# Cross-attention and FFN on one core: TensorE's program without alignment, v of the first pair and the FFN's weights in other space at other times, last pairs in another order

## What is computed

```python
def attn(hidden_q, hidden_kv, mask, position_bias, Wq, Wk, Wv, Wo):
    q = (hidden_q @ Wq).reshape(b, lq, h, dh)
    k = (hidden_kv @ Wk).reshape(b, lk, h, dh)
    v = (hidden_kv @ Wv).reshape(b, lk, h, dh)
    score = einsum('bqhd,bkhd->bhqk', q, k) / sqrt(dh) + position_bias
    probs = where(mask, softmax(where(mask, score, -inf)), 0)
    return einsum('bhqk,bkhd->bqhd', probs, v).reshape(b, lq, h * dh) @ Wo

def ffn(x, base_W, base_b, router_W, router_b, A, B, expert_map):
    base_out = x @ base_W.T + base_b
    probs = softmax(x @ router_W.T + router_b)
    topk_p, topk_i = top_k(probs, 8)
    w = einsum('btk,btke->bte', topk_p, expert_map[topk_i] == arange(8))
    h = einsum('btd,erd->bter', x, A)
    return base_out + 2 * einsum('bter,eor->bto', h * w[..., None], B)

x = x + attn(layernorm(x), ctx, ...)
x = x + ffn(layernorm(x), ...)
```

## Time and profile before

| | |
|---|---|
| three runs, us | 788.65, 790.44, 790.91 (median 790.44) |
| the profiled execution | 791.96 |
| its span, first to last instruction | 790.1 |
| TensorE matmuls, weight loads | 780.8 us (99%), 652.0 us (83%) |
| VectorE, ScalarE, GpSimd | 521.5 (66%), 399.9 (51%), 185.3 (23%) |
| chain that ended last | TensorE 93%, DMA 2%, VectorE 2%, SyncE's queue 1%, issue 1% |
| TensorE clock granted, mean | 0.998 |
| DMA | 118.40 MB, mean 150 GB/s |
| instruction packets of queue q8 | 52, 0.85 MB |

### The profile page before, as it was taken

The page is one execution under the profiler, slowest core; times in us unless marked ns, Lnnn a source line. Parts: engine busy times, 40 slices in busy tenths (PEclk is TensorE's granted clock), DMA queues, the critical chain, the costliest instruction groups (busy, mean ns, idle before and its releaser), DMA issues.

```text
span 790.1 us, 16795 instructions
## 1 busy us (share of the span) xinstructions
PE 780.8 (99%) x6360; PEld 652.0 (83%) x6360; DVE 521.5 (66%) x951; ACT 399.9 (51%) x1138; POOL 185.3 (23%) x203
## 2 busy tenths in 40 slices
PE   8999999999999999989999999999999999999998
PEld 7888888888888888878888888888888888887886
DVE  6883626267677665577666776676667676657974
ACT  5663525246556555573665456535654466435520
POOL 0225041024333434232222122212211221010200
PEclk9999999999999999999999999999999999999999
DMA  6536773245544547583564355534563355342002
GB/s 226 199 121 220 225 243 138 109 139 159 190 160 159 169 154 215 171 250 111 164 182 135 110 157 161 163 110 130 162 177 115 112 160 176 109 118 83 2 6 103
DMA packets 108078, 118.40 MB, mean 150 GB/s; under 512 B 44239, under 2 KB 77007, under 8 KB 107998
## 3 DMA queue, kind: packets, MB, share of 16 engines
q1 hardware_dynamic: 107998, 117.31, 47.7%
HBM read 81.64 MB, written 35.65 MB: 148 GB/s over the span
## 4 chain that ended last, share of the span: by engine, by line
PE 93%; DMA 2%; DVE 2%; SPq 1%; issue 1%; ACT 0%
PE pY L1393 42%; PE pP L1393 39%; PE pY L1552 4%; PE pO L1577 2%; PE pT_ L1577 2%; PE pS L1562 1%; DMA wv_raw<-in_L_xattn_Wv 1%; PE pO L1393 1%; PE pT_ L1562 1%; DMA v<-v_hbm 1%; DMA k_hbm<-stage 1%; SPq L425 1%; DVE st L980 1%; PE pS L1577 1%; DVE y L1129 0%
## 5 line engine op out<-in xcount | busy, mean ns | idle before, releaser
L1129 DVE TENSOR_TENSOR y<-y,pY 128x512 f32<-128x512 f32 x124 | 84.6, 682 | 24.6 <-PE pY L1393 24.2
L1393 PE MATMUL pY<-wo_hi,oT_hi 128*128 128x512 f32 x248 | 97.4, 393 | 1.2 <-issue 1.2
L1393 PE MATMUL pY<-wo_lo,oT_hi 128*128 128x512 f32 x248 | 97.2, 392 | 0.0
L1393 PE MATMUL pY<-wo_hi,oT_lo 128*128 128x512 f32 x248 | 97.2, 392 | 0.0
L910 DVE TENSOR_TENSOR wk_lo<-wk_raw,wk_hi 128x256 fp32r<-128x256 f32 x96 | 46.7, 487 | 62.2 <-ACT wk_hi L651 61.3
L759 ACT ACTIVATE pr<-pr,mx 128x64 f32<-128x64 f32 x256 | 86.2, 344 | 2.8 <-DVE mx L1146 2.8
L651 ACT CAST wk_hi<-twk 128x256 fp32r<-128x256 f32 x128 | 50.7, 409 | 64.5 <-PE pP L1393 53.6
L1393 PE MATMUL pP<-xo_hi,wk_hi 128*128 128x512 f32 x196 | 78.1, 399 | 0.0
L1393 PE MATMUL pP<-xo_hi,wk_lo 128*128 128x512 f32 x196 | 76.6, 391 | 0.0
L1393 PE MATMUL pP<-xo_lo,wk_hi 128*128 128x512 f32 x196 | 76.4, 390 | 0.0
L584 POOL TENSOR_TENSOR bias<-bias,madd 128x512 f32<-128x512 f32 x32 | 41.5, 1308 | 148.2 <-DMA bias<-in_fside_Bx32xSxS 148.2
(11 more groups left out here) (282 smaller groups left out, 1896.6 us busy)
## 6 DMA issues: line engine op xcount, KB each, us to landing
v_hbm<-stage SPq DMA_DIRECT2D x64, 256.0 KB, 2.3
k_hbm<-stage SPq DMA_DIRECT2D x64, 256.0 KB, 3.6
k<-k_hbm SPq DMA_DIRECT2D x16, 1024.0 KB, 5.1
v<-v_hbm SPq DMA_DIRECT2D x16, 1024.0 KB, 7.0
wk_raw<-in_L_xattn_Wk SPq DMA_DIRECT2D x16, 512.0 KB, 4.4
wo_raw<-in_L_xattn_Wo SPq DMA_DIRECT2D x16, 512.0 KB, 3.7
bias<-in_fside_Bx32xSxS SPq DMA_DIRECT2D x128, 64.0 KB, 3.6
wk_raw<-in_L_xattn_Wq SPq DMA_DIRECT2D x16, 512.0 KB, 4.7
```

The lines of the kernel that those rows point to most:

```text
L1129: nc.vector.tensor_tensor(y[:, t, :], y[:, t, :], src[:, :], ALU.add).then_inc(y_added, 1)
L1393: mm = nc.tensor.matmul(bank_, a, b, start=first and n == 0, stop=last and n == len(terms) - 1, skip_group_check=read_between)
```

## The change

It has four parts. The diff below goes, in order, through the tiles, SyncE, ScalarE (pair 14, then 15), VectorE and TensorE. (1) The five `addr_align` are gone; instead of 14 transposes of 128x128 the second warm-up has 12, and 26 of 32x32. (2) v of the first pair goes to a tile of its own, `v0`, over the context's space (read for the last time by product 4 of QA), so it waits for no store; the FFN's raw weights move to the same space and are loaded in passes 1 to 4 and not in passes 12 and 13 and ahead of pair 0, and VectorE's nine small operations on `mapi` move from pass 0 to pass 3. (3) `make_c21(QB)` stands ahead of `lower_wo(0)` on VectorE. (4) In pair 14 ScalarE's `exp(h + 2, 0)` stands behind its four `o_high`; in pairs 14 and 15 `ffn_weights(4)` and (5), and their splits, stand later.

```diff
+        v0 = at("v0", R0 + 16384, [P, NT, 2 * DH])
+        a_raw = at("a_raw", R0 + 16384, [P, D])
+        r_raw = at("r_raw", R0 + 18432, [NR, D])
+        b_raw = at("b_raw", R0 + 20480, [P, DC, ER])
+        bw_raw = at("bw_raw", R0 + 24576, [P, DC, D])
...
-        bw_raw = at("bw_raw", R1 + 49152, [P, DC, D])
...
-        a_raw = at("a_raw", R4 + 16384, [P, D])
-        r_raw = at("r_raw", R4 + 18432, [NR, D])
-        b_raw = at("b_raw", R4 + 20480, [P, DC, ER])
...
             def load_v(i):
-                sp.dma_start(v[:, :, :], v_hbm[i // 2, :, :, i % 2 * 2 * DH:(i % 2 + 1) * 2 * DH]
+                sp.dma_start((v if i else v0)[:, :, :], v_hbm[i // 2, :, :, i % 2 * 2 * DH:(i % 2 + 1) * 2 * DH]
...
+            sp.wait_ge(prod, DONE[QA, 4])
+            load_v(0)
+            store(QA, 2, c21_made)
             load_wk(QA - 9)
-            store(QA, 2, c21_made)
-            sp.wait_ge(prod, DONE[QA, 4])
-            sp.dma_start(bb[:, :], base_b.partition_broadcast(P)).then_inc(ld_small, 16)
-            sp.dma_start(rb[:, :], router_b.partition_broadcast(P)).then_inc(ld_small, 16)
-            sp.dma_start(mapi[:, :], emap.partition_broadcast(P)).then_inc(ld_small, 16)
-            for i in range(4):
-                sp.wait_ge(put[0][i], 16 * (QA // 2 + 1))
-            load_v(0)
...
                 sp.wait_ge(o_full, 4 * (i + 1))
+                if i == 0:
+                    for n in range(4):
+                        sp.wait_ge(put[0][n], 16 * (QA // 2 + 1))
                 load_v(i + 1)
-                if i == NP - 4:
-                    sp.wait_ge(w_lo[5], NSET - 1)
-                    sp.wait_ge(tw_made, 4 * (NSET - 1))
+                if i == 1:
+                    sp.dma_start(bb[:, :], base_b.partition_broadcast(P)).then_inc(ld_small, 16)
+                    sp.dma_start(rb[:, :], router_b.partition_broadcast(P)).then_inc(ld_small, 16)
+                    sp.dma_start(mapi[:, :], emap.partition_broadcast(P)).then_inc(ld_small, 16)
+                if i == 2:
                     sp.dma_start(a_raw[:, :], a_d).then_inc(ld_a, 16)
                     sp.dma_start(r_raw[:, :], router_W).then_inc(ld_a, 16)
-                if i == NP - 3:
-                    sp.wait_ge(prod, len(ORDER))
+                if i == 3:
                     sp.dma_start(bw_raw[:, :, :], bw_d).then_inc(ld_ffn, 16)
+                if i == 4:
                     for o in range(DC):
...
             turned_p(h + 1)
-            exp(h + 2, 0)
             o_high(h, 0)
             o_high(h, 1)
             o_high(h + 1, 0)
             o_high(h + 1, 1)
+            exp(h + 2, 0)
             exp(h + 2, 1)
...
             wo_high(NP - 1)
-            split_ffn(4)
             turned_p(h + 2)
             turned_p(h + 3)
-            split_ffn(5)
+            split_ffn(4)
             o_high(h + 2, 0)
...
             o_high(h + 3, 1)
+            split_ffn(5)
             split_ffn(6)
...
+            make_c21(QB)
             lower_wo(0)
-            make_c21(QB)
...
-                if i == 0:
+                if i == 3:
                     dve.wait_ge(ld_small, 48)
...
             add_tile(i, 6)
-            split_ffn(4)
             add_tile(i, 7)
             lower_wo(NP - 1)
+            split_ffn(4)
             o_low(h + 2, 0)
...
-            def warm_up(count):
+            def warm_up(count, n=P):
                 for _ in range(count):
-                    nc.tensor.transpose(pY[1][:, 0:P], ident[:, :], ident[:, :])
+                    nc.tensor.transpose(pY[1][0:n, 0:n], ident[0:n, 0:n], ident[0:n, 0:n])
...
             turn_ctx(0, first_turn(0))
-            warm_up(14)
+            warm_up(12)
+            warm_up(26, 32)
             turn_ctx(1, first_turn(1))
...
-                                                  v[rows, t, s * DH + 64 * d:s * DH + 64 * d + 64],
+                                                  (v if h >= 2 else v0)[rows, t, s * DH + 64 * d:s * DH + 64 * d + 64],
...
-            nc.tensor.addr_align(256, offset=142)
             times(QB + 1, 1)
...
-                for p in (1, 2) if i else (2,):
-                    times(n, p)
-                if i % 3 == 2:
-                    nc.tensor.addr_align(256, offset=18)
-                for p in (6, 7):
+                for p in (1, 2, 6, 7) if i else (2, 6, 7):
                     times(n, p)
...
                 times_wo(i, t)
-                if t == 5:
-                    ffn_weights(4)
             turn_p(h + 2)
             turn_p(h + 3)
-            ffn_weights(5)
+            ffn_weights(4)
             times_v(h + 2)
             times_v(h + 3)
+            ffn_weights(5)
             ffn_weights(6)
```

## The result

| | before | after |
|---|---|---|
| median, us (9 runs each) | 790.25 (788.65 to 790.94) | 787.04 (786.22 to 788.36) |
| ratio after to before | | 0.9958, 95% interval 0.9947 to 0.9970 |
| the profiled execution, its span | 791.96, 790.1 | 787.04, 785.3 |
| TensorE matmuls | 780.8 us | 778.7 us |
| instruction packets of q8 | 52 | 51 |

The changed kernel is 3.2 us (0.42%) faster; the forecast was 786.8 (785.0 to 789.3), so the number held. Yet in the profiled pair of traces two of its terms were wrong by more than 1.5 us each, in opposite directions. First the page of the kernel after: its TensorE row answers to the earlier trace rows, and the second line gives the chain that ended last, by engine.

What follows compares the result with a forecast made beforehand. TensorE bounds it, busy 780.8 of 790.1 us. Terms -2.7 + 0.6 + 0.1 - 0.5 - 0.45 = -2.95 give 787.5 from the median, 785.8 if the half-clock stretch goes too; 786.8 taken, range 785.0 to 789.3.

Steps and rivals of the forecast that it cites:

- First pair: Attention of the first head pair: its stops for q, v and code nearly all go, -2.7 us.
- What is late instead is wo_lo: VectorE, first pair: wo_lo 0.7 late, then two w_lo and biased(2); only times_wo(0, 0) waits, cost nothing.
- v's late load: First pair: v's late load, with wo and k, holds up the code fetch; 1.5 of the 2.82 us lost.
- No alignment: Loop pairs without padding: stops in regions 3, 6, 9, 12 grow from 1.2 to 1.8 us together, +0.6.
- 5.4 to 5.8: Sign that the slots are right: regions 3, 6, 9, 12 take this many us, all others 5.16.
- The slower rival: Loop regions: boundaries drift, fetch falls behind k's 1 MB load, six stops of 1.53 us, 794.3; chance 0.05.
- 0 to +0.5: Moved loads of the FFN's weights: cost 0, their packets could at most meet one code fetch, at this cost in us.
- Last pairs: Pairs 14 and 15: -0.5 us from idle before times_wo in 14, -0.45 from four transposes in 15.
- the four transposes: Pair 15: they leave the time ahead of the times_wo run and enter its idle part, -0.45 us.
- The half clock: Stretch in pair 14 costing 1.7 us, expected to go more often than not; rival that it stays, chance 0.12.
- Warm-up: Second warm-up: 26 transposes of 32x32 at 32 ns replace two of 128x128; cover used up, +0.1 us.
- the first product at 7.5 to 7.6: Sign for the warm-up: TensorE's first product starts at this time in us.

Runs made afterwards that it cites:

- e1: Changed kernel with the split of Wo ahead of make_c21(QB) on VectorE again, as before the change: 786.89 us.
- e2: Changed kernel with the split of Wo for pair 0 moved behind the lo parts of o in pass 0: 786.72 us.
- e4: Changed kernel with the five alignments and the old second warm-up (14 transposes of 128x128) back: 787.48 us.
- e10: Changed kernel with the loads of the FFN's weights back in passes 12 and 13, behind their old waits: 787.12 us.
- e5: Kernel before with only v of the first pair in free space (v0), loaded ahead of the last store and load_wk(23): 789.44 us.
- e11: Kernel before with v0 and with make_c21(QB) ahead of the split of Wo: 789.35 us.
- e7: Kernel before with only the changed order of pairs 14 and 15 on ScalarE, VectorE and TensorE: 789.16 us.
- e8: Kernel before with one edit: in pair 14 ScalarE's four casts of o stand ahead of the first four exponentials: 789.25 us.
- e3: Changed kernel with make_c11 ahead of the lo parts of o on VectorE in pass 0: 787.23 us.
- e12: Changed kernel with Wo's split behind the lo parts of o and ScalarE's casts of o ahead of exp(2, 0), both in pass 0: 786.80 us.
- e6: Kernel before with the five alignments taken out and nothing else: 795.09 us.
- e9: Changed kernel, still without alignment, with the old second warm-up (14 transposes of 128x128): 788.25 us.

## Why the prediction was right, and where it was not

**First pair: -2.7 predicted, -1.04 in the traces.** The region came as forecast (5.16, no waits for q and v, no stop). The step that failed is "What is late instead is wo_lo ... I cost that at nothing". I named two w_lo and biased(2) behind it, but let only times_wo(0, 0) wait for them, 4 us after the region. I did not follow biased on to largest, and through ScalarE's exponentials and casts to `make_c11`, which TensorE wants 2.8 us after the region. As long as region 0 lost 2.8 us, that piece had cover. The 1.66 are 0.23 that the shorter region alone leaves uncovered (e1, e2), about 0.33 for the moved split by itself (e4, e10) and 1.1 for GpSimd's overlap, into which the moved split pushes the lo parts (e2). Without the overlap, as in e10, pair 0 is 1.95 shorter than before, and the term is off by 0.75. The overlap I could have seen: the earlier trace rows has the split of Wo at 1.76 us, and here it takes 1.22.

The Trainium skill, SBUF — State Buffer, SBUF: two separate sides, says that a VectorE operation with two SBUF inputs and a GpSimd operation hold the shared ports in turn and block each other. The traces agree: 0.95 to 0.97 beside GpSimd and 0.42 without.

**"So I put 1.5 of the 2.82 down to v's late load": half wrong.** v0 alone left a stop of 1.45 (e5). What frees the packet is an idle stretch of the DMA engines where it is due: behind v, and ahead of Wo and k. The order of make_c21 (e11) makes that stretch, since Wo's next load waits for the split and k stands behind it in the queue. The slot does it too: at 207 the packet is due at +0.7 to +1.1, ahead of them (e1, with the old order, is clean). The changed kernel has both, and v0.

**No alignment: +0.6 predicted, -1.05 in the pair of traces.** Regions 3, 6, 9 and 12 took 5.23, 5.15, 5.15 and 5.28, not the 5.4 to 5.8 named as a sign, and no other region of the loop over 5.16. The slots were as worked out: over all traces stops stand only in regions that a second crossing falls into or just behind. The sizes were not: the term took 0.3 at slot 181 and 8 ns more per slot, from one execution. In six aligned traces (before, e4, e5, e7, e8, e11) the excess is 0.77 to 1.42, mean 1.10; in six with the new slots (after, e1, e2, e3, e10, e12) 0.23 to 0.97, mean 0.54. So the term is about -0.6, with the sign wrong. It is the new warm-up's slots that win it, and not the missing padding as such: without alignment but with the old warm-up (e6, e9) the excess is 1.66 and 1.46. With idle DMA engines (96 crossings) a packet starts between 0.4 us before and 1.3 us behind the crossing and takes 0.9 to 1.4, and in 33 stops of the fourteen traces the block ran 1.2 to 1.6 us after the packet's end. A dense block lasts about 3.0 us at slot 181 (from 75 instructions behind the region's start to 331), so the same slot stops for 0 to 0.65. The Trainium skill, Runtime: NRT & Kernel Launch, Instruction fetch mechanics, holds crossings to be mostly hidden. That is so among the wide products, where a block is 128 matmuls 0.23 apart, 29 us; these regions are the exception.

**The slower rival had its place wrong, and its size right by chance.** I gave 794.3 for lost alignment, through k's load in six pairs. Alignment alone taken out gives 795.09 (e6), through one pair, 14, and the FFN's B. I priced a fetch that meets the FFN's packets at "0 to +0.5": with the loads at their old time and the region in that slot it is 2.3 of stop and then half clock. At their new time the loads cost nothing that the traces show, as forecast. Alignment can go only together with the early loads or with the new warm-up's slots.

**Last pairs.** The idle and the four transposes went as worked out (-0.5 and -0.45 predicted). From region 14's start to the first times_wo pass 6.98 us instead of 7.70, so 0.7 of the 2.75 in the traces; the four transposes are 0.5 (from there to pair 15, 12.48 in e8 and 11.98 in e7). The half clock went "more often than not": it never came again. The rest of the 2.75 is that stretch, eight matmuls 0.16 to 0.20 longer, 1.5. The median of before mostly lacks it, so it moves the median little.

**Warm-up.** +0.1 predicted, with the first product at 7.5 to 7.6. It starts at 7.95:

```profile
7.95 0.47 PE L1395 MATMUL pP<-wv_hi,co_hi 128*128 128x512 f32 x1
```

Part of that is no matter of the small transposes: the 128x128 ones ahead of them start 213 ns apart up to 6.1, and 109 only from 6.25 (from 5.22 in the kernel before), so the clock rose later here. Over the traces the first product starts from 7.50 to 8.81 with the new warm-up and from 7.51 to 8.47 with the old. In the pair of traces region 0 starts 0.04 earlier all the same, and by kernel its start scatters from 342.96 to 344.89, so this term can't be confirmed. The small transposes start 29 ns apart (32 was taken), and the clock did not fall behind them.

So the time came out right by luck: in the pair of traces the two big misses cancel, 1.66 less from the first pair and 1.65 more from the alignment. Both sizes belong to these two executions; by the means over the traces the second is 1.2, and without the overlap the first is 0.75.

## What to carry to other kernels

When a stop is removed, list everything that is made in its shadow, on every engine behind the moved instruction, and not only the consumer of that instruction. Where TensorE runs through a block of 256 instructions in some 3 us, its code packet needs idle DMA engines at the crossing; look at what is loaded there before moving either code or loads, and try padding and load times together. A stop that varies from 0 to 0.65 at one place is read from several executions or not at all.

## What the runs showed of the hardware that I had not expected

- An idle of 0.64 us behind a few small transposes goes with a half-clock stretch of about 3.5 us in 2 of 5 runs; without the idle none came in 74.
- One 16 KB code packet amid small data packets came 3.5 us after its crossing, where with idle engines it comes at most 1.3 behind, and TensorE stood 2.3 us.
- From the end of a code packet to the first instruction behind it pass 1.2 to 1.6 us, in each of 33 stops.
- Two VectorE subtractions took 0.95 and 0.97 us beside GpSimd's sums, 0.42 without; and TensorE's wait at the end of the chain was 1.1 us longer.
